# Expert layers of a mixture-of-experts model: the seven small slots set between the sixteen large ones, in a written-out loop

## What is computed

```python
# layer 0
weights, sel = jax.lax.top_k(softmax(x @ router_w.T), 2)
ys = jax.vmap(lambda w1e, w2e: jax.nn.gelu(toks @ w1e) @ w2e)(w1, w2)
out = zeros.at[token_idx].add(ys[expert_flat, arange] * gate[:, None])
# layer 1
h = jax.nn.relu(jnp.einsum('td,ehd->teh', xf, W1) + b1)
y = jnp.einsum('teh,edh->ted', h, W2) + b2
moe = jnp.einsum('te,ted->td', gates, y)
out = moe + 0.1 * K * sh          # sh: the shared expert
```

## Time and profile before

| | |
|---|---|
| median of three runs | 1083.06 us (1082.98 to 1085.27) |
| profiled execution, own time | 1086.5 us |
| its span in the trace | 1084.7 us |
| TensorE busy | 712.0 us (66% of the span), 6945 matmuls |
| VectorE busy | 737.0 us (68%) |
| ScalarE busy | 643.3 us (59%) |
| GpSimd busy | 346.5 us (32%) |
| mean granted TensorE clock | 0.742 of full speed |
| slot work of layer 0, start of the first turn to start of the last add | 487.19 to 635.23 us |
| slot work of layer 1, the same | 927.79 to 1079.57 us |

### The profile page before, as it was taken

The page is one execution under the profiler, slowest core; times in us unless marked ns, Lnnn a source line. Parts: engine busy times, 40 slices in busy tenths (PEclk is TensorE's granted clock), DMA queues, the critical chain, the costliest instruction groups (busy, mean ns, idle before and its releaser), DMA issues. The chain is left out here.

```text
span 1084.7 us, 19299 instructions
## 1 busy us (share of the span) xinstructions
PE 712.0 (66%) x6945; PEld 525.5 (48%) x6946; DVE 737.0 (68%) x1429; ACT 643.3 (59%) x1170; POOL 346.5 (32%) x261
## 2 busy tenths in 40 slices
PE   2167647144189522119999839685787589899985
PEld 1136414022067412118999725332455348799984
DVE  3017799999888888994444446497888987344443
ACT  1015695699968554525555528765995473566664
POOL 6700064000000000025777633376000301277764
PEclk9558855555589865558999978855556699899999
DMA  3001368000055103843333354546000761133332
GB/s 100 10 1 32 108 189 252 11 8 15 0 205 166 39 0 110 288 146 73 59 61 55 45 157 178 197 172 245 4 2 1 268 256 55 42 55 58 58 46 33
DMA packets 61591, 103.12 MB, mean 95 GB/s; under 512 B 9646, under 2 KB 43586, under 8 KB 61522
## 3 DMA queue, kind: packets, MB, share of 16 engines
q1 hardware_dynamic: 45138, 85.67, 23.5%
q0 software_dynamic: 16384, 16.53, 10.0%
HBM read 74.29 MB, written 27.87 MB: 94 GB/s over the span
## 5 line engine op out<-in xcount | busy, mean ns | idle before, releaser
L2026 PE MATMUL m_pu<-m_xgT,m_w 128*128 128x256 f16 (+1 forms) x1380 | 140.9, 262 | 2.7 <-DVE m_xgT L2149 2.6
L2026 PEld LDWEIGHTS m_pu<-m_xgT,m_w 128*128 x1380 | 119.7, 100 | 17.6 <-DVE m_xgT L2149 3.5
L2045 PE MATMUL m_py<-m_w,m_hT 128*128 x1404 | 126.0, 247 | 2.8 <-issue 1.5
L2045 PEld LDWEIGHTS m_py<-m_w,m_hT 128*128 128x128 f16 x1404 | 117.0, 98 | 4.1 <-issue 2.4
L2149 DVE COPY m_xgT<-m_px 128x768 f16<-128x768 f16 (+1 forms) x46 | 22.9, 497 | 125.3 <-PE m_px L1994 125.3
L2116 ACT ACTIVATE m_pu<-m_pu,m_b,m_unit 128x256 f32<-128x256 f32 (+1 forms) x138 | 63.4, 507 | 60.3 <-PE m_pu L2026 57.8
L970 ACT ACTIVATE a_ex<-a_v,a_nb 128x256 bf16<-128x256 f16 x192 | 94.3, 493 | 5.4 <-DVE a_nb L996 5.4
L2157 DVE SCALAR_TENSOR_TENSOR m_hT<-m_pu,m_unit,m_hT 128x512 f16<-128x512 f32 (+1 forms) x138 | 86.3, 663 | 15.6 <-ACT m_hT L2109 15.1
L807 PE MATMUL a_pp<-a_room 16*128 16x256 bf16 x240 | 56.1, 412 | 39.8 <-DVE a_v L984 31.9
L2109 ACT ACTIVATE m_hT<-m_pu,m_unit 128x512 f16<-128x512 f32 (+1 forms) x138 | 81.4, 634 | 0.0
L1960 POOL DMA_INDIRECT m_xg<-xn_d,m_token x70 | 69.8, 997 | 34.7 <-issue 20.3
(11 more groups left out here) (440 smaller groups left out, 1697.2 us busy)
## 6 DMA issues: line engine op xcount, KB each, us to landing
a_room<-in_m_w SPq DMA_DIRECT2D x8, 768.0 KB, 4.4
m_stage<-in_m_w SPq DMA_DIRECT2D x8, 768.0 KB, 5.1
hv_raw<-in_m_w SPq DMA_DIRECT2D x8, 768.0 KB, 7.3
w1h_d<-hv_parts SPq DMA_DIRECT2D x8, 768.0 KB, 4.0
m_w<-w1h_d SPq DMA_DIRECT2D x8, 768.0 KB, 8.8
a_room<-in_m_w SPq DMA_DIRECT2D x8, 576.0 KB, 3.8
m_stage<-in_m_w SPq DMA_DIRECT2D x8, 576.0 KB, 5.3
hv_raw<-in_m_w SPq DMA_DIRECT2D x8, 576.0 KB, 6.3
```

Of the source, the lines that this page charges most:

```text
L2026: last = nc.tensor.matmul(pu[:, u, q // 2, (q % 2) * w:(q % 2 + 1) * w], w1_bytes[:, bass.ds(e * (2 * W) + up_place(wpart, tail, q), 2 * P ...
L2045: last = nc.tensor.matmul(py[:, j * D:(j + 1) * D], hT[:, u, hpart, q * w + j * P:q * w + (j + 1) * P], w2_bytes[:, bass.ds(e * (2 * FC * ...
```

## The change

The slots are done in the order of a table, `ORDER`: small slots 16 to 22 stand behind large ones, the first behind the third large one, the next behind the sixth, and the other five behind every second. The position s in this order takes the place of the slot's number in every wait, buffer and count; `owner`, `token` and `share` are still read by the slot's number. All loops are written out on TensorE, ScalarE and VectorE, and each slot's expert is loaded in front of its up; `load_small` is gone. No arithmetic is added or removed.

```diff
-            def moved(i, u):
-
-                return i * 32 + 32 if large(i, u) else 16 * BIG + 16 * ((2 * i + u - BIG) // 2 + 1)
-
-            def columns(m):
+            ORDER = [0, 1, 2, 16, 3, 4, 5, 17, 6, 7, 18, 8, 9, 19, 10, 11, 20, 12, 13, 21, 14, 15, 22]
+
+            def columns(s):
+
+                m = ORDER[s]
                 return (2 * m, 2 * m + 1) if m < BIG else (BIG + m,)
+
+            def wide(s):
+                return P * len(columns(s))
+
+            def moved(s):
+
+                return 16 * sum(len(columns(z)) for z in range(s % 2, s + 1, 2))
...
-                    with pe.Fori(1, BIG // 2 - 1) as i:
-                        step(i, 0)
-                        step(i, 1)
-                    for m in range(BIG - 2, MAXT):
-                        step(m // 2, m % 2)
+                    for s in range(MAXT):
+                        if s + 1 < MAXT:
+                            up(s + 1, expert(s + 1))
+                        if s + 2 < MAXT:
+                            turn_rows(s + 2)
+                        down(s, bounded(s))
...
-                    with act.Fori(2, BIG // 2) as i:
-                        for u in range(2):
-                            hidden(i, u)
-                    for m in range(BIG, MAXT):
-                        hidden(m // 2, m % 2)
+                    for s in range(MAXT):
+                        hidden(s)
...
-                    with dve.Fori(1, BIG // 2 - 1) as i:
-                        step(i, 0)
-                        step(i, 1)
-                    for m in range(BIG - 2, MAXT):
-                        step(m // 2, m % 2)
+                    for s in range(MAXT):
+                        if s + 2 < MAXT:
+                            rows(s + 2)
+                        if s + 1 < MAXT:
+                            hidden(s + 1)
+                        result(s)
```

More of the change, by code:

```diff
@@ L1981, in _, with turn_rows @@
                         following.reduce(pool)
-                    for m in (MAXT - 2, MAXT - 1):
-                        pool.wait_ge(stored[m % 2], moved(m // 2, m % 2))
+                    for s in (MAXT - 2, MAXT - 1):
+                        pool.wait_ge(stored[s % 2], moved(s))
                 @block.tensor
                 def _(pe):
[L1987 to L1991, removed]
+                    def turn_rows(s):
+                        w, u = wide(s), s % 2
+                        pe.wait_ge(got[u], moved(s))
+                        if s > 0:
+                            pe.wait_ge(xkept, s)
                         for j in range(w // P):
@@ L2031, in up, with down @@
                                 last.then_inc(upped, 1)
-                    def down(i, u, e):
-                        w = 2 * P if large(i, u) else P
+                    def down(s, e):
+                        w, u = wide(s), s % 2
                         down_addresses(e)
-                        pe.wait_ge(lowered[u], i + 1)
-                        if not (isinstance(i, int) and i == 0 and u == 0):
-                            pe.wait_ge(out, i * 2 + u)
+                        pe.wait_ge(lowered[u], s // 2 + 1)
+                        if s > 0:
+                            pe.wait_ge(out, s)
                         for j in range(w // P):
@@ L2053, in _ @@
                     experts_of = [pe.alloc_register(f"{L}_expert{u}") for u in range(2)]
[L2054 to L2082, removed]
@@ L2159, in hidden, with result @@
                         last.then_inc(lowered[u], 1)
[L2161 to L2188 removed]
+                    def result(s):
+                        u = s % 2
+                        dve.wait_ge(downed[u], s // 2 + 1)
+                        if s >= 2:
+                            dve.wait_ge(stored[u], moved(s - 2))
+                        for j, n in enumerate(columns(s)):
+                            last = v.tensor_scalar(yo[:, u, j, :], py[:, j * D:(j + 1) * D], share[:, n:n + 1], None,
+                                                   ALU.mult)
+                        last.then_inc(out, 1)
+                    rows(0)
+                    rows(1)
+                    hidden(0)
+                    for s in range(MAXT):
+                        if s + 2 < MAXT:
+                            rows(s + 2)
+                        if s + 1 < MAXT:
+                            hidden(s + 1)
+                        result(s)
                     if following:
```

111 lines of the change are left out of this document (43 added, 68 removed).

## The result

The changed kernel takes 1091.41 us (median of 7 runs, 1090.58 to 1097.31) against 1083.06 us before in the same timing (7 runs, 1082.14 to 1092.53): **slower by 0.72%**, ratio 1.0072 with a 95% interval of 1.0040 to 1.0104. Its profiled run is 1091.41 us too, span 1089.6. The forecast was 1083.7 us, range 1078.5 to 1088.0.

The account below looks back on a forecast made before the run. GpSimd's floor, with TensorE just ahead of it and waiting for gathers, sets the slots: 133.3 against 131.85 us and 134.7 against 135.52, together 0.65 us more. On the 1083.06 us median that gives 1083.7 us, range 1078.5 to 1088.0.

Parts of the forecast that it names:

- The 4.2 us from writing the loops out: Large slots: VectorE's copy, some 1.0 us late at the loop's turn, comes in time; 1.3 and 2.9 us won.
- rival 3: The late VectorE copy stays because it is not the loop's; the 4.2 us don't come, 1087.9 us; chance 0.11.
- The rounds of small, large, large: Middle of each layer's slots: 17.7 us per three slots in layer 0, 17.95 in layer 1; four rounds 70.8 and 71.8.
- the term of 0.3 us from a result to its add: Time from VectorE's result to GpSimd's add, counted as 0.3 us within 9.1 us from a down to a later turn.
- W: Time from the last DMA of an add to the next add on GpSimd, taken as 4.3 us, the small slots' pace.
- rival 2: Adds' DMAs are slower beside gathers, W from 4.6 up: 3.4 us over the sum, 1087.1 us; chance 0.17.
- The order costs time by late gathers: Gathers queued behind adds make TensorE's turns wait near small slots, 0.8 us plus 0.24 of issue; net total 0.65 us more.
- The first seven distances in sum: Add-to-add distances over positions 0 to 7: 45.8 us in layer 0 and 46.2 us in layer 1.
- the last three: Last add-to-add distances of each layer, with no gathers: 4.3 + 6.2 + 6.2 = 16.7 us.
- load_small's gap: The 1.22 us gap ahead of a TensorE down from the small slots' seven register loads goes; counted as 0 gain.
- The small result behind the hidden values: VectorE makes a small slot's result late, behind the next large slot's hidden values; GpSimd idling over a few tenths disproves the prediction.
- GpSimd's floor: GpSimd's minimum for adds and gathers: 127.8 us before, 128.1 after, so no gain; 17.18 us per three slots.

Follow-up runs that it names:

- the 1085 condition: Timings in which the unchanged kernel before took 1083 to 1087 us, on the same chips; ratios are to the kernel before of the same timing.
- the 1045 condition: Timings in which the unchanged kernel before took 1044 to 1045 us, on the same chips; ratios are to the kernel before of the same timing.
- the early gathers: Changed kernel with three buffers for gathered rows in place of two, each gather one slot earlier on GpSimd: 1033.95 us, 0.9867 of the kernel before.

## Why the prediction was wrong

- **The 4.2 us from writing the loops out: this step failed.** I read one late copy as the loop's turn. The kernel before has the same late copies in both looks under the 1085 condition and none at 1045, where it has the forecast pace with its loops; the old order written out is 0.9997 and 1.0005 there, and under the 1085 condition, with the gathers ahead, written-out code and loops are equal (0.9961 and 0.9965). I even had the place wrong: the loop's body starts with the copy of an even slot, and the late copy at 560.20 is slot 11's, mid-body. This is rival 3 in what it costs, to which I gave 0.11, but not in its form: in the trace after the late copies did go (one of 46 is over 0.2 us late), and it won nothing. The Trainium skill (Runtime: NRT & Kernel Launch, Instruction fetch mechanics) had the branch not stall in so short a body, and the runs agree with it: with both loops kept, the copy behind the branch is 0.14 us late and the others 0.04.
- **The rounds of small, large, large: mis-sized, and this is where the changed kernel's own stretches miss.** Forecast were 17.7 and 17.95 us a round, measured 18.7 and 19.2, together 8.7 us over eight rounds; the rest of the two stretches is 125.3 us where the sum had 125.4. Two terms were too small. First, the term of 0.3 us from a result to its add. A small slot's result is ready before the DMAs of the large add in front of it are done, so by my own W its add has to wait (2.06 us at 570.50), and the gather behind it is late for the turn right behind the next small slot. My count had only looked at the turn two positions behind. Second, W = 4.3: six waits of the trace after are over 4.8 us, counted from the start of the last issue, up to 6.40 us at 619.58, all with an instruction packet beside them. That is rival 2 in size (W over 4.6), by another cause than the gathers that I had named. How the 8.7 us divide between the two is not shown.
- **The order costs time by late gathers: right in kind.** I had 0.65 + 4.2 = 4.85 us for it; against the old order written out it is 5.5 us in one timing of the 1045 condition and some 2 in the other, and 5.4 and 4.7 us in the stretches. In one timing the early gathers take the ratio from 1.0019 to 0.9867, so gathers behind adds are the cause there.
- Rivals 2 and 3 were priced each by itself, 1087.1 and 1087.9. The order at 4.85 us without the loops' 4.2, and W's 3.4 on top, gives 1083.06 + 4.85 + 3.4 = 1091.3 us; measured 1091.41. That they meet so well is luck: in the 1045 condition the loss is 0.2 to 0.6%, and in the trace after the copies came in time while the whole excess stands in the rounds.
- The first seven distances in sum (45.3 and 46.1 us), the last three in layer 0 (16.3; 17.5 in layer 1) and load_small's gap (gone): as forecast. Within the seven two errors cancel in part: small to large takes 5.1 and 5.9 us, not 6.6 and 6.75, and large to small 7.4 and 6.9. The chances for faster, within and slower do not follow from those of the rivals: with a tenth of 0.45 on either side they would be 0.32, 0.36 and 0.32. The small result behind the hidden values, which I had named as what would prove me wrong, was not the cause: moving it won nothing. GpSimd's floor did not fall, as forecast; the time of three slots once the gathers are early, 17.0, is the floor of 17.18.

What stays open: why the 1085 condition has late starts on VectorE and ScalarE, and how much of the 8.35 us there is packets and how much is order. The old order written out, with its gathers where they were, was never run in that condition.

## What to carry to other kernels

Where slots of different size are mixed, a queue that issues gathers behind adds must run further ahead: a short slot takes away the time that hid the gather. Count for the small slot too what its add waits for, not only when its result is ready. Look for the place in the queue before adding a buffer. And a delay seen in one execution is no property of a loop until a second look has it too; price rivals that can both be true together as well.

## What the runs showed of the hardware

- Instruction packets are counted on the same 16 DMA engines as indirect DMAs: 12 of 16 KB in a layer's slots when TensorE's loop is written out, 6 when it isn't. All 48 waits on an add of over 3.2 us have one beside them. That written-out code costs time by it is not shown: the old order written out is 0.9997 and 1.0005 of the kernel before.
- Under the 1085 condition copies start up to 4.3 us behind their turn (at 995.15 in the second run of two buffers with gathers ahead), and GpSimd's adds seem to have a part: 11 of 12 copies over 0.3 us late in the kernel before start 1.30 to 1.42 us into an add's DMA instruction of 1.56 to 1.62 us. The Trainium skill (SBUF — State Buffer, section SBUF: two separate sides) says that GpSimd shares a port pair with VectorE's operations in a two-port mode or with two SBUF inputs, and that the pair is held for a whole instruction. These copies have one input, in PSUM, and no run shows whether they take the pair; if they did, they would start at the add instruction's end, which they do not; and in the 1045 condition none of 51 copies that became ready in the first 0.4 us of an add was late, in eight traces. So it is not shown.
- Most of the 40 us between the conditions lies ahead of the slots, from 20 to 75 us, where the kernel before moved 7 GB/s in one and 37 in the other. Busy times of this stretch, columns as in the earlier trace rows, first under the 1085 condition:

```profile
20.00:75.00 55.00, 19.64 (x60) 8.53 (x59) 4.87 (x13) 3.23 (x6) 27.46 (x30) 0.56 0.06 7
```

and under the 1045 condition:

```profile
20.00:75.00 55.00, 48.34 (x237) 32.81 (x235) 30.66 (x88) 23.09 (x48) 28.52 (x29) 0.78 0.18 37
```

In both, GpSimd issues one indirect DMA after another there. The same VectorE instruction, which waits for a TensorE result (by the profile there at 25.1 us and at 35.1), starts at once under the 1045 condition. Under the 1085 condition VectorE sits idle for 21.71 us before it, till after the last of GpSimd's issues:

```profile
25.17 0.34 DVE L667 TENSOR_SCALAR o<-po,bl 64x128 f32<-64x128 f32 x1 [1.00 <-PE po L459]
55.35 0.94 POOL L375 DMA_INDIRECT a_v<-in_p,idx  x1 [0.31 <-issue]
63.03 0.34 DVE L667 TENSOR_SCALAR o<-po,bl 64x128 f32<-64x128 f32 x1 [21.71 <-remote]
```

(the first row is of the 1045 condition, the other two of the 1085 condition). So these late starts and those of the copies may be of one kind, beside GpSimd's indirect DMAs; this is seen in traces and no run tests it.
